# A mixture-of-experts block moved into the next batch's first attention, and the first batch's scores placed beside its key projections

## What is computed

```python
# layer 0: attention over all 2304 tokens of the group-normed image, plus a squeeze-and-excite branch
g = group_norm(x)                                 # 32 groups of 4 channels
q, k, v = Wq@g + bq, Wk@g + bk, Wv@g + bv
attn = softmax(q.T @ k)                           # 2304 x 2304 a batch
x = x + gamma * (v @ attn) + g * sigmoid(se_w2 @ relu(se_w1 @ mean(g)))
# layer 1, on tokens
t = tokens(x);  n = layer_norm(t)
t = t + softmax(n @ n.T) @ n                      # second attention
u = layer_norm(t)
p = softmax(u @ router_w + router_b)              # 8 experts, the best 2 kept and rescaled
t = t + sum of the 2 kept experts' (u @ expert_w[e] + expert_b[e]) * p[e]
```

## Time and profile before

| | |
|---|---|
| median of 3 runs | 2722.33 us (2719.2 to 2723.67) |
| profiled execution, its own time | 2717.11 us |
| its span in the trace | 2715.1 us |
| granted clock, mean | 0.994 |
| PE busy | 2591.4 us |
| DVE busy | 2135.2 us |
| ACT busy | 1952.5 us |
| POOL busy | 475.8 us |
| chain that ended last | PE 76%, DVE 11%, ACT 8%, issue 3%, POOL 2% |

### The profile page before, as it was taken

The page is one execution under the profiler, slowest core; times in us unless marked ns, Lnnn a source line. Parts: engine busy times, 40 slices in busy tenths (PEclk is TensorE's granted clock), DMA queues, the critical chain, the costliest instruction groups (busy, mean ns, idle before and its releaser), DMA issues.

```text
span 2715.1 us, 46080 instructions
## 1 busy us (share of the span) xinstructions
PE 2591.4 (95%) x15334; PEld 2377.9 (88%) x15334; DVE 2135.2 (79%) x6216; ACT 1952.5 (72%) x3732; POOL 475.8 (18%) x840
## 2 busy tenths in 40 slices
PE   6999999999999999999999999999999999999996
PEld 5889888898888988889888898888989889888995
DVE  6886778877788787887878877888778887788675
ACT  4668776677776777677866778667776677766774
POOL 0000220023101231012300123002230022300234
PEclk9999999999999999999999999999999999999998
DMA  1000000000000000000000000000000000000000
GB/s 38 1 19 1 7 7 1 19 7 7 7 1 18 7 10 4 1 19 7 9 4 1 21 4 9 4 1 21 7 10 1 1 21 7 10 1 1 7 7 12
DMA packets 11321, 23.15 MB, mean 9 GB/s; under 512 B 1360, under 2 KB 7760, under 8 KB 11088
## 3 DMA queue, kind: packets, MB, share of 16 engines
q1 hardware_dynamic: 11088, 20.20, 2.1%
HBM read 10.76 MB, written 9.44 MB: 7 GB/s over the span
## 4 chain that ended last, share of the span: by engine, by line
PE 76%; DVE 11%; ACT 8%; issue 3%; POOL 2%; DMA 0%; ACTq 0%; SPq 0%; DVEq 0%; POOLq 0%
PE ps L1071 21%; PE ps L1073 21%; PE ps L1072 20%; PE ps L1084 13%; DVE pt_lo L970 2%; ACT row_space L695 2%; ACT row_space L649 2%; ACT pt_hi L704 2%; DVE u_tok L947 1%; DVE pt_lo L896 1%; ACT row_space L729 1%; DVE gn_raw L768 0%; POOL acc L578 0%; DVE acc L1054 0%; DVE t_tok L914 0%
## 5 line engine op out<-in xcount | busy, mean ns | idle before, releaser
L660 ACT ACTIVATE pt_hi<-ps 128x384 fp32r<-128x384 f32 x864 | 419.1, 487 | 346.5 <-PE ps L1084 346.4
L896 DVE TENSOR_TENSOR pt_lo<-ps,pt_hi 128x384 fp32r<-128x384 f32 x864 | 475.0, 554 | 180.5 <-ACT pt_hi L660 166.7
L695 ACT ACTIVATE row_space<-ps,shift 128x768 f32<-128x768 f32 x432 | 390.2, 903 | 226.5 <-PE ps L1073 216.1
L970 DVE TENSOR_TENSOR pt_lo<-row_space,pt_hi 128x768 fp32r<-128x768 f32 x432 | 420.9, 974 | 151.1 <-ACT pt_hi L704 150.0
L881 DVE TENSOR_SCALAR_CACHE_REDUCE row_space<-ps 128x512 f32<-128x512 f32 (+1 forms) x720 | 452.6, 630 | 24.5 <-PE ps L1073 18.0
L1084 PE MATMUL ps<-ident,row_space 128*128 128x128 f32 x2736 | 446.3, 273 | 17.5 <-ACT row_space L649 16.6
L1084 PEld LDWEIGHTS ps<-ident,row_space 128*128 128x128 f32 x2736 | 347.9, 140 | 108.1 <-ACT row_space L649 29.9
L649 ACT ACTIVATE row_space<-row_space,negmax 128x512 f32<-128x512 f32 (+2 forms) x432 | 402.8, 933 | 36.2 <-DVE negmax L890 35.9
L704 ACT ACTIVATE pt_hi<-row_space 128x768 fp32r<-128x768 f32 x432 | 365.6, 846 | 40.4 <-PE ps L1073 1.1
L1071 PE MATMUL ps<-pt_hi,v_hi 128*128 128x384 f32 x864 | 352.0, 407 | 8.2 <-ACT y_out L669 7.6
L1071 PE MATMUL ps<-pt_hi,tn_hi 128*128 128x384 f32 x864 | 292.2, 338 | 15.7 <-ACT y_out L669 9.7
(11 more groups left out here) (166 smaller groups left out, 5169.2 us busy)
## 6 DMA issues: line engine op xcount, KB each, us to landing
x_chan<-x SPq DMA_DIRECT2D x24, 384.0 KB, 3.9
y<-y_out SPq DMA_DIRECT2D x48, 192.0 KB, 1.9
t_tok<-eb SPq DMA_DIRECT2D x1, 516.0 KB, 5.1
t_tok<-ew SPq DMA_DIRECT2D x1, 516.0 KB, 5.9
row_space<-wqkv SPq DMA_DIRECT2D x1, 192.0 KB, 3.3
se_sb<-se SPq DMA_DIRECT2D x1, 68.0 KB, 4.2
biases<-channel SPq DMA_DIRECT2D x1, 2.0 KB, 4.5
```

The costliest lines, as they stand in the source:

```text
L660: act.activation(pt_hi[:, slot, :], ring_bank(step)[:, 0:BW], ACT.Copy)\
L695: act.activation(p1_f[:, w % 2, :].rearrange("p (s w) -> p s w", s=2), ps[:, 2 * (w % 2):2 * (w % 2) + 2, 0:BW], ACT.Exp, bias=shift[:, :])\
L896: dve.tensor_tensor(pt_lo[:, slot, :], ring_bank(step)[:, 0:BW], pt_hi[:, slot, :], ALU.subtract).then_inc(pt_lo_ready, 1)
L970: dve.tensor_tensor(p1_lo[:, w % 3, :], p1_f[:, w % 2, :], p1_hi[:, w % 3, :], ALU.subtract).then_inc(p1_lo_ready, 1)
```

## The change

Three things are done, and every engine executes the same operations on as many numbers as before; only the order and some buffers change.

1. *Block 4.* Its mixture of experts leaves the second stage of the next batch and is laid into blocks 1 to 4 of the next batch's first attention (`EARLIER_BLOCK`). As the terms' buffers are in use by block 5 and 0 then, its terms live in `x_chan`, the image's buffer, whose base tiles are taken earlier (`BASE_TILES`); its output has its own use of `y_out` (`out_buffer`), and SP stores it and loads the next image after it.
2. *The next image.* Statistics and normalised image of batch b+1 (`IMAGE`) move from the second stage into blocks 5 and 6 of batch b's first attention. The tables of the second stage are written anew: projections start at slot 1 (before: 10), the first scores at 12 (before: 25), both last value products and their eviction stand in slot 0, and at the slots where a query block's output opens, `SOON` steps come ahead of the product.
3. *The first batch.* Scores of its first row stand beside the key projections, each waiting only for its own part of keys, value products only for their part of values; squeeze-and-excite comes later; `fold`, `foldsplit` and `base` move to block 1 (`FIRST_BLOCK`).

```diff
@@ -46,6 +46,17 @@
+EARLIER_BLOCK = {1: {9: [('uln',)], 10: [('uapply',)], 15: [('ut',)]}, 2: {8: [('router',)], 10: [('gates',)]},
+                 3: {6: [('expert', 0)], 7: [('scaled', 0)], 12: [('expert', 1)], 13: [('scaled', 1)]},
+                 4: {7: [('expert', 2)], 8: [('scaled', 2)], 15: [('yt',)]}}
+BASE_TILES = {(1, 9): [0], (2, 10): [1], (3, 9): [2], (3, 12): [3], (4, 11): [4], (4, 12): [5]}
+IMAGE = {(5, 1): [('stat', 0)], (5, 6): [('stat', 1)], (5, 7): [('stat', 2)], (5, 10): [('stat', 3)], (5, 13): [('stat', 4)],
+         (6, 0): [('stat', 5)], (6, 3): [('gn_mean',)], (6, 5): [('gn_dev',)], (6, 7): [('gn_var',)], (6, 9): [('gn_norm',),
+         ('xgnorm', 0)], (6, 11): [('se_in',)], (6, 13): [('xgnorm', 1)], (6, 16): [('se_out',)], (6, 17): [('xgnorm', 2)]}
@@ -61,29 +72,31 @@
     row = n * TPB + j // 6
+    scores = [("score", b, n, row % TPB, k)] if n < NB and k < len(QC) else []
+    if n < NB and k == len(QC) - 1:
+        scores.append(("row_max", b, n, row % TPB))
+    if j == NT - 2:
+        s += scores
...
-    if n >= 1 and j == 9:
-        s.append(("baset", b, n - 1))
+    s += [("baset", b, m) for m in BASE_TILES.get((n, j), [])]
...
-        s += {4: [("ot", b, n - 2)], 15: [("tnt", b, n - 2)]}.get(j, [])
-    products = values(b, n, j)
-    if j < NT - 2:
-        s += products
-    if n < NB and k < len(QC):
-        s.append(("score", b, n, row % TPB, k))
-    if n < NB and k == len(QC) - 1:
-        s.append(("row_max", b, n, row % TPB))
-    if j >= NT - 2:
-        s += products
+        s += {4: [("ot", b, n - 2)], 13: [("tnt", b, n - 2)]}.get(j, [])
+    if n == 1 and not b:
+        s += [(kind, 0, *more) for kind, *more in FIRST_BLOCK.get(j, [])]
+    s += values(b, n, j)
+    if j != NT - 2:
+        s += scores
...
-    if n == NB and b:
-        s += {7: [("uln", b - 1, 4)], 13: [("uapply", b - 1, 4)]}.get(j, [])
+    if n in EARLIER_BLOCK and b:
+        s += [(kind, b - 1, 4, *more) for kind, *more in EARLIER_BLOCK[n].get(j, [])]
+    if b + 1 < B:
+        s += [(kind, b + 1, *more) for kind, *more in IMAGE.get((n, j), [])]
@@ -113,17 +123,17 @@
-MOE_SLOTS = [(None, 0, 2, range(4, 10), 11), (6, 10, 11, range(13, 19), 20), (21, 23, 24, range(26, 32), 33),
...
-STATISTICS_SLOTS = [0, 0, 2, 2, 4, 4, 5, 6, 7, 8, 9, 12]
-NORMALISE_SLOTS = [8, 9, 11]
-PROJECT_SLOTS = {10: [("xg", 0)], 11: [("xg", 1)], 12: [("kproj", 0)], 13: [("xg", 2), ("kproj", 1)],
...
-                 30: [("vproj", 5)], 34: [("base", 2)], 53: [("qproj", 1)]}
-EARLY_SLOTS = [([25, 25, 26, 27, 28], 29, [30, 32, 33]), ([31, 32, 34, 34, 35], 36, [39, 41, 42]),
...
+MOE_SLOTS = [(5, 9, 11, [13, 13, 15, 16, 17, 18], 21), (21, 24, 26, [28, 29, 31, 31, 32, 33], 35), (31, 34, 35,
...
+O1_SLOTS = [20, 29, 38, 40]
+PROJECT_SLOTS = {1: [('xg', 0)], 2: [('xg', 1)], 3: [('kproj', 0)], 4: [('xg', 2)], 5: [('kproj', 1)], 6: [('kproj', 2)],
+                 7: [('kproj', 3)], 8: [('kproj', 4)], 9: [('kproj', 5)], 10: [('qproj', 0), ('vproj', 0)],
+                 12: [('vproj', 1)], 16: [('base', 0)], 18: [('vproj', 2)], 19: [('vproj', 3), ('qproj', 1)],
+                 20: [('vproj', 4), ('vproj', 5)], 21: [('base', 1)], 35: [('base', 2)]}
+EARLY_SLOTS = [([12, 14, 15, 16, 17], 18, [19, 21, 22]), ([21, 21, 23, 23, 24], 25, [25, 26, 27]), ([25, 26, 27, 27, 30], 31,
+               [32, 34, 37])]
@@ -148,16 +158,22 @@
+FIRST_BLOCK = {0: [("fold", 0)], 1: [("fold", 1)], 2: [("fold", 2)], 4: [("foldsplit",)], 5: [("base", 0)],
+               7: [("base", 1)], 9: [("base", 2)]}
...
-    s += [("xgnorm", 0, 0), ("xg", 0, 0), ("xgnorm", 0, 1), ("kproj", 0, 0), ("xg", 0, 1), ("kproj", 0, 1), ("xgnorm", 0, 2),
-          ("kproj", 0, 2), ("xg", 0, 2), ("qproj", 0, 0), ("kproj", 0, 3), ("kproj", 0, 4), ("kproj", 0, 5)]
-    rest = {1: [("gn_norm", 0)], 2: [("se_in", 0)], 3: [("se_out", 0)], 5: [("fold", 0, 0)], 7: [("fold", 0, 1), ("base", 0, 0)],
-            9: [("fold", 0, 2)], 11: [("foldsplit", 0)], 13: [("base", 0, 1)], 15: [("base", 0, 2)]}
-    merge(rest, {slot: [("vproj", 0, m)] for m, slot in enumerate([0, 2, 4, 8, 12, 16])})
-    merge(rest, {j: attention0(0, 0, j) for j in range(NT)})
-    return s + [step for j in range(NT) for step in rest[j]]
+    s += [("xgnorm", 0, 0), ("xg", 0, 0), ("xgnorm", 0, 1), ("kproj", 0, 0), ("xg", 0, 1), ("qproj", 0, 0), ("kproj", 0, 1),
+          ("xgnorm", 0, 2), ("kproj", 0, 2), ("xg", 0, 2), ("kproj", 0, 3), ("score", 0, 0, 0, 0), ("kproj", 0, 4),
+          ("score", 0, 0, 0, 1), ("kproj", 0, 5), ("score", 0, 0, 0, 2), ("score", 0, 0, 0, 3), ("score", 0, 0, 0, 4),
+          ("row_max", 0, 0, 0), ("exp", 0, 0, 0, 0)]
+    rest = {8: [("gn_norm", 0)], 10: [("se_in", 0)], 13: [("se_out", 0)]}
+    merge(rest, {j: [("vproj", 0, m)] for j, m in {5: 0, 6: 1, 7: 2, 8: 3, 10: 4, 12: 5}.items()})
+    return s + [step for j in range(len(QC), NT)
+                for step in (attention0(0, 0, j) if j > len(QC) else []) + rest.get(j, [])]
@@ -192,13 +205,17 @@
             s.append(("s1", b, w))
+        steps = beside.get(w, [])
+        first = [step for step in steps if step[0] in SOON and w < end - LAG]
+        opens = (w - LAG) % NT == 0
+        if opens:
+            s += first
         if LAG <= w < end + LAG:
...
                 s.append(("o1evac", b, (w - LAG) // NT))
-        steps = beside.get(w, [])
-        first = [step for step in steps if step[0] in SOON and w < end - LAG]
-        s += first
+        if not opens:
+            s += first
         if w < end:
@@ -265,10 +282,11 @@
+        if (kind, step[-1]) == ("s1", 0):
+            free = [i for i in free if i >= RING0]
...
-            free = [i for i in free if i not in taken]
@@ -481,6 +503,13 @@
+        def term_of(m, k, i):
+            if m == 4:
+                return x_chan[:, (k % 2 * 5 + i) * 128:(k % 2 * 5 + i + 1) * 128]
+            return terms[:, (m + k) % 2, i, :]
@@ -514,18 +543,21 @@
                 sp.wait_ge(y_chan_ready, at(y_chan_ready, "yt", b, mb))
-                sp.dma_start(y[b, :, mb * BW:(mb + 1) * BW], y_out[:, mb % 2, :]).then_inc(y_stored[mb % 2], 16)
+                sp.dma_start(y[b, :, mb * BW:(mb + 1) * BW], y_out[:, out_buffer(mb), :]).then_inc(y_stored[out_buffer(mb)], 16)
...
+                    if b:
+                        sp.wait_ge(tile_added, at(tile_added, "scaled", b - 1, 4, TPB - 1))
...
-                    store(b - 1, 4)
...
+                if b + 1 < B:
+                    store(b, 4)
@@ -734,12 +766,12 @@
-                        act.wait_ge(y_stored[mb % 2], 16 * (b * (NB // 2) + mb // 2))
-                    if mb == 4 and b + 1 < B:
+                        act.wait_ge(y_stored[out_buffer(mb)], 16 * (b * (NB // 2) + mb // 2))
+                    if mb == 5 and b + 1 < B:
...
-                    act.activation(y_out[:, mb % 2, :], ring_bank(step)[:, 0:BW], ACT.Identity,
+                    act.activation(y_out[:, out_buffer(mb), :], ring_bank(step)[:, 0:BW], ACT.Identity,
@@ -834,7 +866,7 @@
-                        dve.wait_ge(ring_full, filled(("pt", b - 1, NB - 1, NT - 1)))
+                        dve.wait_ge(ring_full, filled(("pt", b - 1, NB - 2, NT - 1)))
@@ -867,9 +899,9 @@
                     dve.wait_ge(ring_full, filled(step))
-                    if n == 0 and r == TPB - 1 and c == 0:
-                        dve.wait_ge(xg_hi_ready, at(xg_hi_ready, "xg", b, LB - 1))
-                        dve.wait_ge(xg_lo_ready, at(xg_lo_ready, "xg", b, LB - 1))
+                    if n == 0 and r == 0:
+                        dve.wait_ge(xg_hi_ready, at(xg_hi_ready, "xg", b, (a + w - 1) // LW))
+                        dve.wait_ge(xg_lo_ready, at(xg_lo_ready, "xg", b, (a + w - 1) // LW))
                     if n == 1 and r == 0 and c == 0 and b:
@@ -1147,10 +1179,10 @@
                         pe.wait_ge(q_lo_ready, at(q_lo_ready, "qproj", b, n))
-                        if n == 0:
-                            pe.wait_ge(k_lo_ready, at(k_lo_ready, "kproj", b, NB - 1))
+                    a, w = QC[c]
+                    if n == 0 and r == 0:
+                        pe.wait_ge(k_lo_ready, at(k_lo_ready, "kproj", b, (a + w - 1) // BW))
                     wait_ring(step)
-                    a, w = QC[c]
                     tile = slice(r * 128, (r + 1) * 128)
@@ -1165,10 +1197,10 @@
                             pe.wait_ge(o_chan_ready, at(o_chan_ready, "oevac", b, n - 1))
-                        else:
-                            pe.wait_ge(v_lo_ready, at(v_lo_ready, "vproj", b, NB - 1))
-                            if b:
-                                pe.wait_ge(o1_chan_ready, at(o1_chan_ready, "o1evac", b - 1, LB - 1))
+                        elif b:
+                            pe.wait_ge(o1_chan_ready, at(o1_chan_ready, "o1evac", b - 1, LB - 1))
+                    if n == 0 and j % TPB == 0:
+                        pe.wait_ge(v_lo_ready, at(v_lo_ready, "vproj", b, j // TPB))
```

33 lines of the change are left out of this document (15 added, 18 removed).

## The result

The changed kernel takes 2656.27 us (median of 4 runs, 2655.72 to 2657.66), the kernel before, run beside it, 2720.76 (2718.92 to 2723.67): ratio 0.976, 95% interval 0.9746 to 0.978. The direction was right, the size off by a factor of nearly two.

The account below looks back on a forecast made before the run. PE was taken as the bound, so only its gaps could shrink: −36.6 − 2.8 − 4.7 + 17.2 − 7.4 = −34.3, from 2722.3 to 2688 us; own range 2668 to 2706, wider range 2664 to 2711.

Parts of the forecast that it names:

- six steady second stages: Second stage: PE's waits fall from 9.6 to 3.5 us, saving 6.1 in each of six, 36.6 in all.
- batch 0's stage: Second stage of batch 0: no block 4 before it and less than half the gap, so 2.8 us saved.
- last stage and tail: Last batch's second stage: ut stands three slots behind its norm, saving 4.7 us; the tail keeps its order.
- seven first attentions: First attention: moved DVE work costs PE 1.6 plus 0.85 us in each of seven batches, 17.2 in all.
- start: First batch up to and with block 1: earlier first transposes and kept clock, less folds in block 1, net 7.4 us saved.
- forecast wait for pt_lo: Draining block of the first attention: gn_mean and gn_dev ahead of a pt_lo pair make PE wait 0.85 us more.
- A: Rival, first attentions: moved DVE work finds no idle time, 8.4 us each instead of 2.45, slower at 2730; chance 5%.
- B: Rival, second stage: gaps mostly come back in the crowded slots, 7.5 us remaining rather than 3.5, 2712; chance 12%.
- D: Rival, first attentions: block 4's loads and store hold up statistics or yt by 3 us and more, cancelling the gain; 3%.
- C: Rival, first attention: it absorbs all, and earlier scores at slot 16 remove the block waits, 2657; chance 12%.
- point of decision: First attention: the change turns slower overall from a cost of 7.4 us a batch.
- gap of 1 us: Start, ahead of the first transposes: PE idles only about 1 us, so the clock stays and 2.6 us are saved.

Follow-up runs that it names:

- slot-0 edit: Kernel before, with the first attention's last value product and its eviction moved from slot 1 to slot 0 of the second stage: 2722.15 us against 2717.13, ratio 1.0011.
- dosing run: Changed kernel with 1 to 8 extra DVE statistics, results unused, in each of blocks 2 and 5 of batches 1 to 6's first attentions: 2680.74 us (one run).

## Why the prediction was right in direction and wrong in size

The prediction's terms beside the traces' lost time, in us:

| term | forecast | measured |
|---|---|---|
| six steady second stages | −36.6 | six stages of about 4.1 − 12.8: −52.2 |
| batch 0's stage | −2.8 | −5.7 |
| last stage and tail | −4.7 | −8.3 |
| seven first attentions | +17.2 | +9.7 (steady: 6.3 − 5.0 each) |
| start | −7.4 | −4.2 (medians: −5.5 to −6.0) |
| sum | −34.3 | −60.7 |

**The steps that failed are the sizes of two terms, the stage's and the attention's**: a steady stage was to save 6.1 us and saved 8.7, an attention was to cost 2.45 and cost 1.3. The mechanism held: PE's gaps in the second stage close, DVE has room for most of what moves. The ends of the range didn't cover it: the lowest that the stage's term allowed was 1.5 left of 9.6, a saving of 8.1, below what was measured. The stated ends also can't be added up from their terms (−12 and −7 give 2669, +18 and +7 give 2713, where 2668 and 2706 stand).

*Second stage.* Of the 2.6 us missed in each, some 1.3 are waits that I kept in the new order at 3.5 us and that came to 2.2: at the products 3, 5 and 6 I took 1.0, 0.4 and 0.2 (rows 0.63, 0.52 and none), at slots 19 to 21 0.8 (0.23), at a query block's start 0.75 (0.50), for the rest 0.3 (0.35, for yt 5); these were worked out from the order with durations, at places for which no row stood. 0.4 is the waits of before, 10.0 instead of 9.6. The last 1.0 is delays below 0.17 us, which print as no idle at all: 2.8 in a stage before, 1.8 after. I had no term for them. This last part is the least certain: counted with the product ahead as part of the kind, it is 2.8 and 2.6, and the stage's saving 8.3 instead of 8.7. That closing one wait isn't worth its size was missed the other way: the slot-0 edit, priced at 1.4 a batch, gives nothing on the old kernel. My reading, which no run isolates, is that the ends of ACT's and DVE's work in slots 0 to 5 set the time there. The sum came out too small all the same: with block 4 back in those slots a cycle is 4.5 us longer.

*Batch 0 and the last stage.* I took the first at under half of a steady one from its idle time of 4.30; by lost time it had 9.2. In the last I counted ut's three waits and 0.6 beside them; yt's (1.38, 0.60 and 0.56 of lost time) and the 1.5 of the first value product went too.

*First attention.* 2.45 a batch was forecast, 1.3 measured. Block 1's norm and transposes cost nothing (0.5 forecast), router and gates 0.7 (1.0), the draining block 0.45 (0.85), block 5 0.2 (0.1). In the draining block the forecast wait for pt_lo didn't come, and its printed idle is 1.11 us, where it was 1.03 before; by the other count it cost nothing. The place of the router's delay was wrong: it shows first at slot 13's transposes, whose tokens' `lnapply` stands behind the gates, and only at the next opening when the gates are moved behind it. With the two parts 15 slots apart it costs nothing. That earlier scores at slot 16 give back next to nothing was right: the five openings lose 0.38 in place of 0.43 each.

*Rivals.* A is out (1.3 us an attention, not 8.4), B is out (4.1 left in the stage, not 7.5), and so is D: in the changed kernel no wait of the attention and stage of batch 3 is for a transfer. C named the right time (2657) for half the right reason, which is luck: the attention took nearly all, but the openings kept their waits, and the rest came from the stage. A's mechanism, every us of added DVE work felt, is real, but only from where the change stops: the dosing run shows it from the next 0.46 us on. That its point of decision was not reached I put down to two things, neither tried by itself: PE gains 7.5 us of products in the attention (156.71 busy against 149.23) while DVE gains 10.2 of work, and blocks 1 and 2 had 4 to 5 us free.

*Start.* The forecast had PE idle for about 1 us ahead of the first transposes at 42.3; it idles for 3.36 until 44.4. Its last score starts at 40.57, as forecast (40.9), but its eviction starts only at 42.92, since DVE has the low halves of a value and a query projection up to 40.1 and then squeeze-and-excite ahead of the third row's last evictions:

```profile
40.66 0.15 DVE L850 TENSOR_SCALAR gs<-gs 128x1 f32<-128x1 f32 x1
...
41.49 0.16 DVE L861 TENSOR_TENSOR gs<-gs,biases 128x1 f32<-128x1 f32 x1
41.69 0.69 DVE L913 TENSOR_SCALAR_CACHE_REDUCE row_space<-ps 128x512 f32<-128x512 f32 x1
...
42.92 0.42 DVE L913 TENSOR_SCALAR_CACHE_REDUCE row_space<-ps 128x256 f32<-128x256 f32 x1
```

```profile
44.44 0.90 PE L1116 MATMUL ps<-ident,row_space 128*128 128x128 f32 x3 [3.36 <-ACT row_space L681]
```

```profile
44.72:48.20 3.48, 3.48 (x11) 2.23 (x11) 1.37 (x3) 2.04 (x3) 0.00 (x0) 0.59 0.00 0
48.20:54.00 5.80, 5.80 (x36) 4.79 (x35) 5.23 (x14) 2.46 (x6) 0.00 (x0) 1.00 0.00 0
```

The clock falls to 0.59 for 3.5 us behind the shorter gap too, 1.4 us of the 2.6 that I had counted as saved. The Trainium skill (TensorE: Matmul & The Clock Gate, "What's actually happening") has the throttle as the default, released by activity; the trace agrees with it, with 0.59 behind a gap of 3.36. The gap of 1 us that the forecast took for harmless never occurred, so it was the gap's length that failed, and no run shows what one of that length does there.

**What stays open.** The parts of the retimed tables other than block 4 (the cycle's 331.2 to 329.3 with image, slot 0 and spacing all in) were tried only together, and block 4's move only on top of them. Why the old start is released late in some executions is not settled.

## What to carry to other kernels

Price a gap by the distance of starts, not by printed idle time, and add the delays too short to print: here they were 2.8 us of a stage's 12.8. A wait that one edit removes can come back a few steps later: it did so in full with the value product in slot 0, in greater part with DVE's statistics gone as well, and in greater part with the gates one slot later. So don't add up the waits that an edit removes; try it, and measure the cycle. Where work moves to an engine with room on average, split its chains and keep them ahead of nothing that is needed within the next slots: router and gates together cost 0.7 us a batch, apart nothing.

## What the runs showed of the hardware

The granted clock prints as 1.00 at a program's beginning while products run at half rate (128-column products 0.21 us apart instead of 0.11, up to 40 to 41 us in three of five traces with the old start, 77 to 79 products); the rows show it, not the clock's column. The Trainium skill, in the same section, calls the number of slow products at a kernel's start variable from run to run; the traces agree, with 19 and 34 products ahead of the release in two traces of the old start and 77 to 79 in the other three. And waits of PE in the midst of a busy stretch can lower the clock or not, and their length doesn't decide it: 2.80 and 1.20 us of idle close together gave 0.60 for 3.3 us, 0.51 and 1.19 gave 0.55 for 3 us, and 1.88 and 1.20 between them kept 1.00. What does decide it no run here shows.
